# Negated score tiles in SBUF for the row minimum and the squares of a language-model tower's attention

## The reference

```python
attn1 = jax.nn.softmax(jnp.einsum('bhqd,bhkd->bhqk', q1, k1) * scale, axis=-1)
attn2 = jax.nn.softmax(jnp.einsum('bhqd,bhkd->bhqk', q2, k2) * scale, axis=-1)
...
        mean = r.mean(axis=(-1, -2))
        std = jnp.std(r, axis=-1, ddof=1).mean(axis=-1)
        mx = r.max(axis=-1).mean(axis=-1)
        mn = r.min(axis=-1).mean(axis=-1)
...
fused = alpha_full * attn1 + (1.0 - alpha_full) * attn2
out = jnp.einsum('bhqk,bhkd->bhqd', fused, v)
```

## Time and profile before

| | |
|---|---|
| median of three runs | 6056.63 us |
| lowest, highest | 6050.68, 6056.67 us |
| the profiled execution: span from its first to its last instruction | 6159.6 us |
| busy share: PE, DVE, ACT, POOL | 86%, 83%, 84%, 40% |
| mean granted TensorE clock | 0.942 |

### The profile page before, as it was taken

The page is one execution under the profiler, slowest core; times in us unless marked ns, Lnnn a source line. Parts: engine busy times, 40 slices in busy tenths (PEclk is TensorE's granted clock), DMA queues, the critical chain, the costliest instruction groups (busy, mean ns, idle before and its releaser), DMA issues.

```text
span 6159.6 us, 116651 instructions
## 1 busy us (share of the span) xinstructions
PE 5323.7 (86%) x34070; PEld 2463.4 (40%) x34070; DVE 5116.9 (83%) x5665; ACT 5198.9 (84%) x7937; POOL 2450.5 (40%) x4439
## 2 busy tenths in 40 slices
PE   6988989889898988889889898988889889898985
PEld 4443424334343443434334343443434334343442
DVE  1988889888888988889888888988888888888982
ACT  2988889889898988889889897888888889898884
POOL 6525344352433425344252433425344252433422
PEclk8999999999999999999999999999999999999997
DMA  1001010010101001010010101001010010101000
GB/s 38 19 21 26 18 28 20 21 26 22 26 19 27 20 20 26 19 28 19 21 26 22 26 19 27 20 21 26 22 26 18 22 25 22 26 19 27 20 21 12
DMA packets 164901, 140.60 MB, mean 23 GB/s; under 512 B 89197, under 2 KB 108269, under 8 KB 164141
## 3 DMA queue, kind: packets, MB, share of 16 engines
q1 hardware_dynamic: 159100, 124.09, 8.8%
q0 software_dynamic: 4352, 8.92, 0.7%
q10 hardware_dynamic: 816, 0.02, 0.0%
HBM read 21.26 MB, written 8.91 MB: 5 GB/s over the span
## 4 chain that ended last, share of the span: by engine, by line
PE 54%; issue 14%; DVE 13%; ACT 10%; POOL 5%; SPq 1%; another core or an unknown queue 1%; ACTq 0%; DMA 0%; DVEq 0%; POOLq 0%
PE ps_w L387 21%; PE ps_t L387 11%; PE ps_o L387 11%; PE ps_s L387 10%; DVE rowmin L715 7%; ACT junk L577 4%; DVE negmax L710 4%; ACT exps L583 2%; SPq L328 1%; DVE bn L727 1%; ACT hpre L632 1%; DVE o_raw L723 1%; ACT stage L587 1%; POOL part L855 1%
## 5 line engine op out<-in xcount | busy, mean ns | idle before, releaser
L710 DVE TENSOR_REDUCE negmax<-ps_s 128x1 f32<-128x1024 f32 x2048 | 2491.5, 1217 | 805.8 <-PE ps_s L387 695.9
L577 ACT ACTIVATE junk<-ps_s,negmax 128x1024 bf16<-128x1024 f32 x2048 | 2295.5, 1121 | 288.8 <-DVE rowmin L715 278.3
L715 DVE TENSOR_REDUCE rowmin<-ps_s 128x1 f32<-128x1024 f32 x2048 | 2486.7, 1214 | 0.0
L583 ACT ACTIVATE exps<-ps_t 128x1024 f32<-128x1024 f32 x2060 | 2122.3, 1030 | 314.3 <-PE ps_t L387 173.6
L387 PE MATMUL ps_s<-kst,qst 96*128 96x512 bf16 x4096 | 1293.8, 398 | 520.7 <-ACT junk L577 461.4
L387 PE MATMUL ps_o<-exps,v_cur 128*32 128x256 f32 x16512 | 1381.8, 408 | 159.5 <-DVE o_raw L723 130.0
L387 PE MATMUL ps_t<-qst,kst 99*128 99x512 bf16 x4120 | 1305.8, 400 | 85.8 <-ACT exps L583 70.4
L387 PE MATMUL ps_w<-xc,cw 128*128 128x256 f32 x4704 | 1178.6, 387 | 0.0
L387 PEld LDWEIGHTS ps_w<-xc,cw 128*128 128x128 f32 x4704 | 914.3, 195 | 215.4 <-issue 9.5
L855 POOL TENSOR_SCALAR ctmp<-ug 128x256 f32<-128x256 f32 x408 | 165.8, 406 | 1602.8 <-ACT ug L652 1587.4
L387 PEld LDWEIGHTS ps_s<-kst,qst 96*128 96x128 bf16 x4096 | 343.8, 100 | 1106.8 <-ACT junk L577 828.0
(11 more groups left out here) (179 smaller groups left out, 3902.4 us busy)
## 6 DMA issues: line engine op xcount, KB each, us to landing
qst<-part SPq DMA_DIRECT2D x1542, 32.0 KB, 2.0
kst<-part SPq DMA_DIRECT2D x1542, 32.0 KB, 2.0
qst<-mrow SPq DMA_DIRECT2D x1028, 1.5 KB
out_dram<-z SPq DMA_DIRECT2D x17, 512.0 KB, 3.2
fc1s<-in_fc_w SPq DMA_DIRECT2D x17, 256.0 KB
fc2s<-in_fc_w SPq DMA_DIRECT2D x17, 256.0 KB
cw<-in_conv_w SPq DMA_DIRECT2D x1, 2304.0 KB
odif<-in_table,idx POOLq DMA_INDIRECT x136
```

The source lines that it names most:

```text
L577: nc.scalar.activation(junk[:, n % 2, :], ps_s[:, n % 2, :], ACT.Exp, bias=negmax[:, r, t:t + 1], accum_out=sumsq[:, r, t:t + 1]).then_inc ...
L583: nc.scalar.activation(exps[:, n % RING, :], ps_t[:, :, :].rearrange("p c q -> p (c q)"), ACT.Exp, scale=0.5).then_inc(s_exp, 1)
L710: nc.vector.tensor_reduce(negmax[:, r, t:t + 1], ps_s[:, n % 2, :], axis=AX, op=ALU.max, negate=True)\
L715: nc.vector.tensor_reduce(rowmin[:, r, t:t + 1], ps_s[:, n % 2, :], axis=AX, op=ALU.min)\
```

## The change

The row maximum becomes one DVE instruction that multiplies the score tile by -1, writes the product to one of four new SBUF tiles (`neg_s`, f32) and accumulates its minimum, which is the negated maximum, into `negmax`. The row minimum becomes a negated maximum over the SBUF tile of the step before (tile n - 1, modulo 128), behind a wait for that tile's maximum; one more of them follows the loop. The squares read the SBUF tile, with a scale of -1, and wait for the maximum of their own tile. `scores(n)` waits for `row_max(n - 2)`. In exchange, `row_max(n)` waits for `squares(n - 4)`, the last reader of its SBUF tile. The unit's statistics on POOL wait for the last row minimum as well. To make room, `hid1` and `hid2` lie in tiles that are free at that time, and the DMA scratch is 4096 instead of the default size.

```diff
+SLOTS_S = 4
...
+        neg_s = sb("neg_s", [P, SLOTS_S, L])
...
-        hid1 = sb("hid1", [P, 2, T * NW])
-        hid2 = sb("hid2", [4 * HD, 2, T * NW])
+        hid1 = gtmp[:, :, :].rearrange("p (a b) c -> p a (b c)", a=2)
...
+        hid2 = x2[0:4 * HD, 0:4, :].rearrange("p (a b) c -> p a (b c)", a=2)
...
-                pe.wait_ge(s_sq, i * STEPS + n + 1)
+                pe.wait_ge(s_max, i * STEPS + n + 1)
...
-                act.wait_ge(s_min, i * STEPS + n + 1)
-                act.wait_ge(s_sq, i * STEPS + n + 1)
-                nc.scalar.activation(junk[:, n % 2, :], ps_s[:, n % 2, :], ACT.Exp, bias=negmax[:, r, t:t + 1],
+                act.wait_ge(s_max, i * STEPS + n + 3)
+                act.wait_ge(s_sq, i * STEPS + n + SLOTS_S - 1)
+                nc.scalar.activation(junk[:, n % 2, :], neg_s[:, n % SLOTS_S, :], ACT.Exp, scale=-1.0,
+                                     bias=negmax[:, r, t:t + 1],
                                      accum_out=sumsq[:, r, t:t + 1]).then_inc(s_sq, 1)
...
-            act.sem_inc(s_sq, 2)
+            act.sem_inc(s_sq, SLOTS_S)
...
                 dve.wait_ge(s_scores, i * STEPS + n + 1)
-                nc.vector.tensor_reduce(negmax[:, r, t:t + 1], ps_s[:, n % 2, :], axis=AX, op=ALU.max, negate=True)\
-                    .then_inc(s_max, 1)
+                dve.wait_ge(s_sq, i * STEPS + n + 1)
+
+                nc.vector.tensor_scalar(neg_s[:, n % SLOTS_S, :], ps_s[:, n % 2, :], -1.0, None, ALU.mult, ALU.min,
+                                        accum_out=negmax[:, r, t:t + 1]).then_inc(s_max, 1)
...
             def row_min(i, n):
-                r, t = n // T % RING, n % T
-                nc.vector.tensor_reduce(rowmin[:, r, t:t + 1], ps_s[:, n % 2, :], axis=AX, op=ALU.min)\
-                    .then_inc(s_min, 1)
+
+                m = (n - 1) % STEPS
+                r, t = m // T % RING, m % T
+                dve.wait_ge(s_max, i * STEPS + n + 2)
+                nc.vector.tensor_reduce(rowmin[:, r, t:t + 1], neg_s[:, m % SLOTS_S, :], axis=AX, op=ALU.max,
+                                        negate=True).then_inc(s_min, 1)
...
+            nc.vector.memset(neg_s[:, :, :], 0.0)
...
+            dve.sem_inc(s_max, 2)
...
+            row_min(NB, 0)
...
-                pool.wait_ge(s_sq, i * STEPS + max(T * (j - 2) + T + 2, 2))
+                pool.wait_ge(s_sq, i * STEPS + max(T * (j - 1), 0) + SLOTS_S)
+                pool.wait_ge(s_min, i * STEPS + max(T * (j - 1), 0) + 1)
...
-                    pool.wait_ge(s_max, i * STEPS + T * j)
+                    pool.wait_ge(s_max, i * STEPS + T * j + 2)
...
-    nc = _bacc.Bacc("TRN2", target_bir_lowering=False, num_devices=1)
+    nc = _bacc.Bacc("TRN2", target_bir_lowering=False, num_devices=1, dynamic_dma_scratch_size=4096)
```

## The result

The changed kernel takes **5975.77 us** (median; 5966.17 to 5978.36), 0.9865 of the time before [0.9852, 0.9877], 81 us less. The forecast was 5991 us, range 5875 to 6105.

What follows compares the result with a forecast made beforehand. No single engine bounds it: a ring of scores, maximum, minimum, squares, with PE-bound and stalled steps. Gain 6.9 less loss 2.7 is 4.2 us per batch element, 67 us: 6092.6 profiled, times 0.9833, 5991 us; range 5875 to 6105.

Steps and rivals of the forecast that it cites:

- The durations: On DVE, scaled copy and SBUF minimum cost what the reductions did; on ACT, squares reading SBUF 13 ns longer.
- Convolution steps: Steps where PE has no gap, 2.95 us each; claimed to stay as they are.
- The places named in the forecast: Layer norms ln2 and ln3, both Gelus, square root, four short DVE-bound runs: gain 6.9 us per batch element.
- 25 x 0.08 + 9 x 0.08 = 2.7: Loss per batch element in us: 25 steps without DVE gap, nine unit-step waits for DVE's transpose, 0.08 each.
- x: Cost per step on DVE of the maximum's accumulated output; taken as 0.08 us, with ends 0 and 0.21.
- Rival 3: Accumulator read on DVE is long, kernel slower; decides from x = 0.18 us; at 0.3, 6127 us; chance 0.19.
- only moved: Rival: in DVE-bound stretches the minimum's pass just changes place, waits shift to maxima; no gain, 6057 us; chance 0.10.
- Square root: Shorter ACT stall, exponential running beside scores and weighted values; gain 0.8 us per batch element.
- First Gelu: Behind this ACT stall transposed scores follow the exponential directly, scores being done during it; gain 1.1 us per batch element.
- The short runs: Four places of DVE-bound steps between convolutions, at half price; gain 2.1 us per batch element.
- The term at the unit steps: PE waits for DVE's transpose of ps_o, x queues ahead: 9 x 0.08 = 0.7 us loss per batch element.
- rival 1: Decoupling goes further: 40% of PE's 461.4 us wait for squares goes, 185 us, to 5875 us; chance 0.13.

Runs made afterwards that it cites:

- the repeated profile of before: The unchanged kernel before, profiled once more beside the experiments; span 6049.3 us, timed 6055.15 us, ratio 0.9997.
- the kernel with exchanged buffers: Changed kernel with the unit's transpose ahead of the minimum, plus one PSUM buffer for scores and two for transposed scores: 6067.56 us, ratio 1.0016.

## Why the prediction was right, point by point

**The durations were right.** Copy and minimum cost what the reductions cost, 1215 ns. The squares became 29 ns longer (1149 against 1120), not 13.

**The sign and most of the mechanism were right.** The squares follow their maximum in 1.24 instead of 2.36 us, and PE's wait became one for the exponential. Convolution steps stayed: 2.84 us from 1957.09 to 1959.93.

```profile
1957.09 1.46 PE L389 MATMUL ps_w<-xc,cw 128*128 128x256 f32 x6
...
1959.93 1.46 PE L389 MATMUL ps_w<-xc,cw 128*128 128x256 f32 x6
```

(This pair, the first of its run of convolutions, lies 2.95 us apart in both profiles of before, as in the earlier trace rows, and 2.84 to 3.88 after; the next pair lies 2.84 apart in both kernels.)

**That the sum came so near, 5991 against 5976 us, is luck.** The places named in the forecast gave 3.5 us per batch element where 6.9 were forecast, and other places, where nothing was forecast, 1.1. The step "25 x 0.08 + 9 x 0.08 = 2.7" had x eight times too large, and 34 steps where the runs show some 60; 60 x 0.01 is 0.6 us. Had x been the 0.08 that I took, 60 steps would have lost 4.8 us, 67 us more in all, and some 14 of the 81 us would have been left. Rival 3's point of decision, 0.18, lies near 0.095 by these runs. (In the same rival 6159.6 + 75 is 6235, not 6231, and the time 6130, not 6127; no other number hangs on it.)

**Nothing on DVE was "only moved".** I took the minimum of the tile before for a reordering. It is what keeps maximum and minimum overlapped: without it the change is 31 us slower than the kernel before.

**The gains at the places named were over-estimated, 6.9 against 3.5.** The 3.5 are a net figure of the table: what x and the unit steps took in the same stretches is already taken off.
- *Square root, 0.8 forecast, nothing found.* It could have been read from the trace of before. There the exponential behind the square root ended at 2009.42 and the transposed scores began 0.25 us later, as in the last 15 batch elements of both profiles, so no more than that was to be had:

```profile
2008.41 1.01 ACT L583 ACTIVATE exps<-ps_t 128x1024 f32<-128x1024 f32 x1
...
2009.67 0.60 PE L387 MATMUL ps_t<-qst,kst 99*128 99x512 bf16 x2
```

- *First Gelu, 1.1 forecast, 0.32 found.* The order came out as forecast: the transposed scores are PE's first matmuls, 0.06 us behind the exponential.

```profile
2149.83 1.00 ACT L586 ACTIVATE exps<-ps_t 128x1024 f32<-128x1024 f32 x1
...
2150.89 1.04 PE L389 MATMUL ps_t<-qst,kst 99*128 99x512 bf16 x2 [5.76 <-ACT exps L586]
...
2151.72 2.77 PE L389 MATMUL ps_w<-xc,cw 128*128 128x256 f32 x6
...
2154.28 1.06 PE L389 MATMUL ps_s<-kst,qst 96*128 96x512 bf16 x2
```

 Before, the same place read:

```profile
2177.38 1.01 ACT L583 ACTIVATE exps<-ps_t 128x1024 f32<-128x1024 f32 x1
2177.53 1.03 PE L387 MATMUL ps_s<-kst,qst 96*128 96x512 bf16 x2 [5.63 <-ACT junk L577]
...
2179.51 1.03 PE L387 MATMUL ps_t<-qst,kst 99*128 99x512 bf16 x2
...
2180.34 1.71 PE L387 MATMUL ps_w<-xc,cw 128*128 128x256 f32 x6
...
2181.89 0.60 PE L387 MATMUL ps_s<-kst,qst 96*128 96x512 bf16 x2
```

 PE comes out of the stall at a granted clock of 0.50 in both (2150.80 to 2155 after, 2177.50 to 2180.70 before). Before, the scores ran at it; now the convolution does, 2.77 us instead of 1.71. The next scores come 3.45 us behind the exponential's end after and 3.50 before. I priced what followed at full clock, although showed 1.03 us for two score matmuls that take 0.60 elsewhere.
- *The short runs*, 2.1 forecast: one of four places gave 0.63, the others nothing.
- *Not forecast:* 0.5 at steps 0 to 12 and 1.06 at steps 113 to 127. The latter stands for the most part in step 127, the last of a batch element, which went from 4.29 to 3.23 us. The run that makes PE wait for squares again loses only 0.26 of the 1.06, so the early release does not make most of it. The lower clock, 3.5 us at 0.50 there in that run against 4.3 before, could make up to half of the 0.80 that is left (an estimate, half of 0.8). The squares behind the maximum remain by elimination alone; why just there was not tested further.

**The term at the unit steps was under-estimated.** I gave it 0.08 x 9, 0.7 us. PE now comes for `o_raw` before DVE has it 180 times instead of 145, and the wait grew from 132 to 241 us; with PE waiting for squares again it is 186, so that half of the growth goes with the early release. Up to 36 us went back there, 2.2 us per batch element. The prediction named this as what speaks against rival 1, and put no price on it: with the transpose ahead in both kernels the change is worth 139 us, where rival 1 had 185.

## What to carry to other kernels

Before pricing a small addition on an engine, count the steps in which that engine is never idle, whatever stands in them, and not by the tasks planned there: in the repeated profile of before DVE is idle for less than 0.05 us in 59 of 128 steps, where I had counted 25. An extra instruction of known pitch, for which nobody waits, measures the count directly. When a chain is shortened, look at what is queued on the same engine ahead of the next consumer: work that nobody awaits (here the minimum) belongs behind work that someone does, and moving it gave 94 us on top of the change's 81, though only 36 in the kernel before. A wait for the instruction just ahead on the same engine isn't free, although the timelines show DVE taking its queue in order: it added 0.12 us to a step here (2.39 against 2.27), so take such an operand one tile late.

## What the hardware showed unexpectedly

- On DVE a short instruction's duration says little of its price: the 83 ns accumulator read and the 65 ns memset added 0.01 us to a step, a reduction of 64 elements with 0.21 us added 0.13, and a wait for the result of the instruction just ahead added 0.12.
- TensorE's granted clock took back gains behind the first Gelu. In the stretch of the changed kernel from 2150.80 on (1.2 us, behind 5.76 us without a matmul) PE ran at a granted clock of 0.50, and from 2156.20 on at 1.00:

```profile
2150.80:2152.00 1.20, 1.11 (x3) 0.75 (x4) 0.00 (x0) 1.20 (x3) 0.56 (x2) 0.50 0.24 55
...
2156.20:2158.00 1.80, 1.80 (x13) 1.40 (x10) 1.54 (x3) 1.03 (x2) 0.00 (x0) 1.00 0.00 0
```

- A stall of PE can cost about as much behind it as in it: behind the 2.92 us in the kernel with exchanged buffers, the next scores, weighted values and transposed scores took 1.04, 1.08 and 1.04 us in place of 0.60, 0.64 and 0.60, and a convolution 2.71 in place of 1.46, at a granted clock of 0.50 from 2098 to 2102. That is 2.6 us more.
